# A planner's choice of PSUM banks and the order of the first loads in a fused three-layer decoder kernel

## The chip, the cores and the metric

One NeuronCore of a Trainium2 chip runs the whole kernel. The metric is the device time of one execution in microseconds (us). Three executions of the kernel before took 1398.2 to 1399.92 us, median 1399.54 us. One further execution was taken with the hardware profiler: 1397.8 us, of which its trace spans 1396.1 us.

The engines are named as in the profile: PE is TensorE (matmuls; PEld its weight loads), DVE is VectorE, ACT is ScalarE, POOL is GpSimd, SP is SyncE, which here only issues DMAs. Each engine works through its own queue in order. They meet at semaphores: every engine counts its finished steps, and another engine waits until that count is reached.

## What is computed

For each of 16 batch items (512 rows of 256 numbers) three blocks are added to the running x:

```python
x = x + nystrom_attention(layernorm(x))        # 16 heads, 64 landmarks
x = x + cross_attention(layernorm(x), ctx, mask) # 16 heads, 64 keys
x = x + expert_ffn(layernorm(x))               # 1 of 8 experts, chosen by the item's last row

# nystrom_attention, per head: q_l, k_l are means over 8 rows each
attn1 = softmax(q @ k_l.T); attn2 = softmax(q_l @ k_l.T); attn3 = softmax(q_l @ k.T)
V = attn2
for _ in range(6):
    KV = attn2 @ V
    V = 0.25 * V @ (13 * I - KV @ (15 * I - KV @ (7 * I - KV)))
out = attn1 @ (V @ (attn3 @ v))

# expert_ffn
h = gelu(x @ W1[sel] + b1[sel]); y = h @ W2[sel] + b2[sel]
x = x + 0.3 * (y @ Wo + bo)
```

All of it is in float32. The products W2[e] @ Wo of the eight experts are formed once at the start (the "fusion", steps `f.0` to `f.7` and `fb`) and stored to memory.

## The kernel before, in words

The work is cut into named steps, each belonging to one engine and one batch item. A step's name has its kind and indices: `t1.1` is the second half of the scores of attention 1, `iT.2`, `iZ.2`, `jT.2`, `jZ.2` are the four matmul groups of the third of six iterations, `e1.1.3` an exponential of ACT that empties the fourth bank of `t1.1`. Three texts list the order of all steps by hand: `FIRST` for the start, `TURN` for the repeated part, `LAST` for the end. A turn holds the first attention of one item, the cross-attention and the expert of older items, and the projections of the next (the suffix -1, -2, -3 says how far back), so that PE always has another item's work between two dependent steps. `S` steps issue DMAs on SP, `P` steps are PE's, `A`, `D` and `G` those of ACT, DVE and POOL. `program()` unrolls the lists into `PROGRAM`.

PSUM has eight banks of 128 x 512 float32. Every PE step writes 1, 2 or 4 of them (`banks_of`), and a named step of ACT or DVE empties each (`emptied_by`). `plan()` walks through `PROGRAM` once and gives out the banks: a list `free` holds the free banks in the order in which they were emptied, in program order over all engines, and each step takes from the front, `free.pop(0)`. `BEFORE` keeps which step emptied the bank last. In the PE block, `body` turns this into waits: `emptied` is the count of ACT and of DVE that must be reached before the banks may be written, and each kind adds what its operands need, through `due` (operand and bank of one engine in one wait) or `unmet` (operand alone). `first` leaves a wait out where PE has already waited for as high a count of that engine. A step has 0 to 3 waits: 244 steps have none, 596 one, 407 two and 44 three, 1542 waits in all. The first `wait_ge` of a step rides on its first weight load, the others are an instruction of their own ahead of it, which can hold two.

At the start SP issues the first x, then, in the same step `S.x@0`, the four constants of the first layer (`FIRST_CONSTS`: wqkv with 768 KB, bqkv with 3 KB, bv and bout with 128 KB each), then w2.2 (512 KB, one expert's matrix for the fusion), then the fusion's own constants (`fc`: wfo with 256 KB, b2T and bfo with 8 KB each), then the other matrices. PE's first step is `f.2`, which needs w2.2 and `fc`. DVE's step `nmA` of item 0 and POOL's `xr` wait for `FIRST_CONSTS`, and the load of the second x (`S.x@1`) waits for both.

Lines of the profile: matmuls of `chain` are L1322 (projections, fusion, expert), of `spread_out` L1331 (`iT`, `iZ`), of `bring_home` L1341 (`jT`, `jZ`); `t1` and `tx` begin with L1562, `t3` with L1447, `s1` is L1530, `xnTb` and `xnTc` are L1397, `a` is L1477 and L1479. DVE's `wb` is L1152, `recx` the RECIPROCAL L1218, `y` L1182; ACT's `az` is L940, `q` L874, `h` L1006, `e3` L896, `ex` L959; POOL's `kbd` is L691.

Of the kernel before, what the change touches and what calls it, by code (L numbers as in the profile page):

```python
# [13 lines left out]
P = 128  # L14
# [47 lines left out]
    S.x@0 S.w2.2@0 D.lnA@0 S.fc@0 P.f.2@0 S.w2.3@0 S.w2.1@0 P.f.1@0 P.f.3@0 G.lnA@0 D.nmA@0 A.f.2@0  # L62
# [216 lines left out]
def emptied_by(engine, step):  # L279
# [12 lines left out]
    if engine == "D":  # L292
# [10 lines left out]
        if kind in ("v", "s2", "mT3", "z", "o1", "w1", "vx", "ox", "wx", "logit", "y3", "fb"):  # L303
# [4 lines left out]
OPERANDS_FROM = {"q": "A", "k": "A", "v": "A", "s3": "A", "x2T": "D", "mT3": "D", "t3": "AD", "zT": "AD", "z": "A",  # L308
# [3 lines left out]

# [16 lines left out]

def plan():  # L330
# [20 lines left out]
def decoder_kernel(nc, a, out):  # L351
# [9 lines left out]
    with ExitStack() as ctx:  # L361
# [130 lines left out]
        passed = {}  # L492

        def first(eng, sem_, n):

            if passed.get((eng, sem_), 0) >= n:
                return False
            passed[eng, sem_] = n
# [7 lines left out]
        def due(eng, who, emptied, i, *steps):  # L506

            n = max(emptied[who], *[DONE[who, i, s] for s in steps])
            return n if first(eng, done[who], n) else 0
# [136 lines left out]
        def _(pool):  # L646
# [186 lines left out]
            run("G", body)  # L833
# [3 lines left out]
        def _(act):  # L837
# [177 lines left out]
            run("A", body)  # L1015
# [3 lines left out]
        def _(dve):  # L1019
# [291 lines left out]
            run("D", body)  # L1311
# [3 lines left out]
        def _(pe):  # L1315
# [35 lines left out]
            def body(i, step):  # L1351
# [6 lines left out]
                if "D" not in OPERANDS_FROM.get(kind, ""):  # L1358
                    if first(pe, dve_done, emptied["D"]):
                        pe.wait_ge(dve_done, emptied["D"])  # L1360
                if "A" not in OPERANDS_FROM.get(kind, ""):
                    if first(pe, act_done, emptied["A"]):
                        pe.wait_ge(act_done, emptied["A"])
                o = tile(i, step)
                if kind == "kx":
                    all_consts(pe)
                    g = slice(8 * LM * n, 8 * LM * (n + 1))
# [3 lines left out]
                elif kind == "vx":  # L1371
                    all_consts(pe)
                    if first(pe, ctx_loaded, 16 * (i + 1)):
                        pe.wait_ge(ctx_loaded, 16 * (i + 1))
                    for r in range(2):
                        last = chain(o[64 * r:64 * r + 64, 0:P],
                                     [(ctxT[:, k, :], wv[:, k, r * P:(r + 1) * P]) for k in range(KD)])
                elif kind == "xnTa":
                    if i == 0:
                        if c := due(pe, "D", emptied, 0, ("nmA",)):  # L1380
                            pe.wait_ge(dve_done, c)
                    elif c := unmet(pe, "G", i, ("lnA",)):
                        pe.wait_ge(pool_done, c)
                    for t in range(T):
                        last = nc.tensor.transpose(o[:, t * P:(t + 1) * P], xn["a"][:, t, n * P:(n + 1) * P], ident[:])  # L1385
                elif kind in ("xnTb", "xnTc"):
                    x = kind[-1]
                    if x == "b" and n == 0:
                        if c := unmet(pe, "G", i, ("lnB", 0)):
                            pe.wait_ge(pool_done, c)  # L1390
                    else:
                        if c := due(pe, "A", emptied, i, ("nmB",) if x == "b" else ("nmC", n)):
                            pe.wait_ge(act_done, c)
# [291 lines left out]
```

## Time and profile before

| | |
|---|---|
| median of three executions | 1399.54 us (1398.2 to 1399.92) |
| the profiled execution | 1397.8 us, span of its trace 1396.1 us |
| mean granted TensorE clock | 0.998 |
| PE busy | 1355.2 us (97%) |
| PEld busy | 889.7 us (64%) |
| DVE busy | 1029.5 us (74%) |
| ACT busy | 667.0 us (48%) |
| POOL busy | 571.1 us (41%) |
| PE's share of the chain that ended last | 85% |

The page gives one execution. Busy times are the union of an engine's instructions; the ends of matmuls are modelled and overlap the next ones, so a short stall of PE, up to some 0.2 us or more after a matmul of 512 columns, doesn't show as idle time. It shows in the starts: equal steps have equal distances from start to start, and a longer distance is a wait. The timeline merges instructions of one line that follow each other; "x2" with 0.77 us are two instructions that together take 0.77.

### The profile page before, as it was taken

The numbers are of one execution on the slowest core, as the hardware profiler recorded it, in microseconds if no ns is written. First come the engines' busy times: TensorE is split into PE (matmuls) and PEld (weight loads), VectorE is DVE, ScalarE is ACT, GpSimd is POOL, SyncE is SP. The second block draws the span as 40 slices with busy tenths as digits, with TensorE's granted clock in tenths as the row PEclk, the third lists the DMA queues.
The fourth block names the chain that finished last, engine by engine and source line by source line (L and its number), as shares of the span: only waits on it lengthen the run. The fifth ranks groups of instructions, "written<-read, shape, count | busy, mean of one in ns | idle before, by whom it ended". The sixth has DMA issues, their size and how long they took to land.

```text
span 1396.1 us, 53472 instructions
## 1 busy us (share of the span) xinstructions
PE 1355.2 (97%) x23732; PEld 889.7 (64%) x23732; DVE 1029.5 (74%) x2194; ACT 667.0 (48%) x1230; POOL 571.1 (41%) x799
## 2 busy tenths in 40 slices
PE   6998999999999999999999999999999999999998
PEld 4756666666766767665666766666666656676555
DVE  3487887758786886878778686877868777898641
ACT  2424355454555546355554644555454544435652
POOL 6223444443626244362534436153353543417132
PEclk9999999999999999999999999999999999999999
DMA  8002010120201011020101101010110100001122
GB/s 285 1 3 95 3 63 3 45 75 3 66 5 51 20 38 33 3 66 5 51 20 37 34 3 58 13 51 20 37 34 3 52 2 19 18 4 39 25 77 65
DMA packets 40536, 53.18 MB, mean 38 GB/s; under 512 B 9698, under 2 KB 30450, under 8 KB 40306
## 3 DMA queue, kind: packets, MB, share of 16 engines
q1 hardware_dynamic: 31602, 41.37, 9.2%
q10 hardware_dynamic: 8704, 8.39, 1.8%
q8 instruction: 187, 3.06, 0.9%
q14 instruction: 43, 0.35, 0.1%
HBM read 37.16 MB, written 12.59 MB: 36 GB/s over the span
## 4 chain that ended last, share of the span: by engine, by line
PE 85%; DVE 5%; ACT 3%; issue 2%; POOL 1%; DMA 1%; DVEq 1%; POOLq 0%; SPq 0%; ACTq 0%
PE bank L1322 41%; PE bank L1575 8%; PE bank L1341 7%; PE bank L1331 7%; PE bank L1564 3%; PE bank L1530 2%; PE bank L1418 2%; PE bank L1397 2%; PE bank L1462 2%; PE bank L1543 2%; PE bank L1451 2%; ACT p3T L896 1%; PE bank L1385 1%; PE bank L1562 1%; PE bank L1424 1%
## 5 line engine op out<-in xcount | busy, mean ns | idle before, releaser
L778 POOL TENSOR_TENSOR b<-ut,eye 128x256 f32<-128x256 f32 x192 | 137.6, 733 | 498.6 <-DVE ut L1161 428.9
L940 ACT ACTIVATE az<-bank 128x320 f32<-128x320 f32 x192 | 67.5, 400 | 185.6 <-PE bank L1331 185.2
L1322 PE MATMUL bank<-xnT_a,wqkv 128*128 128x512 f32 x256 | 123.6, 609 | 0.3 <-ACT xnT_a L864 0.3
L1218 DVE RECIPROCAL oT_x<-bank 128x256 f32<-128x256 f32 x64 | 109.2, 1733 | 19.2 <-PE bank L1575 19.2
L1322 PE MATMUL bank<-w2e,hT 128*128 128x256 f32 x512 | 119.0, 386 | 1.5 <-ACT hT L1006 1.4
L1218 DVE RECIPROCAL oT<-bank 128x256 f32<-128x256 f32 x64 | 111.5, 1747 | 10.6 <-PE bank L1575 10.6
L1322 PE MATMUL bank<-xnT_c,w1e 128*128 128x512 f32 x256 | 117.0, 597 | 1.3 <-DVE m_x L1192 0.9
L1090 DVE TENSOR_REDUCE m<-bank 128x1 f32<-128x512 f32 x128 | 82.9, 680 | 38.5 <-PE bank L1418 36.9
L1322 PEld LDWEIGHTS bank<-w2e,hT 128*128 128x128 f32 x512 | 96.0, 192 | 16.9 <-issue 2.7
L896 ACT ACTIVATE p3T<-bank 128x512 f32<-128x512 f32 x128 | 66.7, 603 | 79.1 <-PE bank L1451 78.9
L959 ACT ACTIVATE pT_x<-bank,neg_bias 128x512 f32<-128x512 f32 x128 | 79.9, 696 | 29.8 <-PE bank L1564 28.8
L1152 DVE SCALAR_TENSOR_TENSOR wb<-bank,eye 128x256 f32<-128x256 f32 x192 | 73.1, 411 | 28.5 <-PE bank L1331 27.8
L1192 DVE TENSOR_REDUCE m<-bank 128x8 f32<-128x512 f32 x128 | 81.7, 682 | 15.4 <-PE bank L1530 15.2
L1192 DVE TENSOR_REDUCE m_x<-bank 128x8 f32<-128x512 f32 x128 | 79.5, 680 | 14.6 <-PE bank L1543 14.5
L1170 DVE SCALAR_TENSOR_TENSOR uz<-uz,bank 128x320 f32<-128x320 f32 x192 | 78.3, 435 | 8.2 <-PE bank L1341 5.6
L1341 PEld LDWEIGHTS bank<-wb,az 64*64 64x64 f32 x2560 | 45.5, 134 | 57.9 <-DVE wb L1152 43.9
L1006 ACT ACTIVATE hT<-bank,b1e 128x512 f32<-128x512 f32 x64 | 43.2, 683 | 75.8 <-PE bank L1322 75.5
L1322 PEld LDWEIGHTS bank<-xnT_c,w1e 128*128 128x128 f32 x256 | 46.8, 190 | 49.3 <-issue 44.8
L1331 PEld LDWEIGHTS bank<-uz,ut 64*64 64x64 f32 x3072 | 59.2, 133 | 27.8 <-DVE uz L1170 10.9
L958 ACT ACTIVATE pT<-bank 128x512 f32<-128x512 f32 x128 | 68.5, 604 | 16.6 <-PE bank L1564 16.5
L685 POOL TENSOR_SCALAR xn_a<-x_in,mv_a,rstd_a 128x256 f32<-128x256 f32 x60 | 72.8, 1228 | 2.7 <-issue 2.5
L1331 PE MATMUL bank<-uz,ut 64*64 64x80 f32 (+1 forms) x3072 | 71.3, 228 | 1.2 <-DVE attn L1120 0.4
(223 smaller groups left out, 2979.2 us busy)
## 6 DMA issues: line engine op xcount, KB each, us to landing
x_in<-in_x SPq DMA_DIRECT2D x16, 512.0 KB, 3.8
w1e<-in_W SPq DMA_DIRECT2D x16, 512.0 KB, 3.5
w2e<-w2o SPq DMA_DIRECT2D x16, 512.0 KB, 4.1
out<-base ACTq DMA_DIRECT2D x32, 256.0 KB, 2.1
row_e<-w2o_row SPq DMA_DIRECT2D x16, 128.0 KB, 4.6
hT<-in_W2T SPq DMA_DIRECT2D x2, 512.0 KB, 6.5
pT_x<-in_ctxT SPq DMA_DIRECT2D x1, 1024.0 KB
ctxT<-in_ctxT SPq DMA_DIRECT2D x16, 64.0 KB, 2.6
```

The source lines that it names most:

```text
L778: return g.tensor_tensor(b7[:, q, :], ut[:, q, :], eye[28 if it else 7][:].unsqueeze(1) .broadcast_to([P, 4, LM]), ALU.subtract).then_inc( ...
L896: return s.activation(p3T[:, j].rearrange("p t c -> p (t c)"), tile(i, ("t3", k), j)[:], ACT.Exp).then_inc(act_done, 1)
L959: return s.activation(pT[x][:, 4 * k + j, :], src, ACT.Exp, bias=neg_bias[:, i:i + 1]).then_inc(act_done, 1)
L1090: return v.tensor_reduce(m3[:, k, j:j + 1], tile(i, ("s3", k), j)[:], AX.X, ALU.max).then_inc(dve_done, 1)
L1152: return v.scalar_tensor_tensor(wb[:, h], src, 1.0 / 16 if it else 1.0, eye[15][:].unsqueeze(1).broadcast_to([P, 4, LM]), ALU.mult, ALU.ad ...
L1170: return v.scalar_tensor_tensor(uz[:, q, lo:], uz[:, q, lo:], 3.25 if it else 13.0, src[:, :, lo:], ALU.mult, ALU.subtract).then_inc(dve_d ...
L1192: return v.tensor_reduce(m[x][:, :, j, 2 * k:2 * k + 2], tile(i, ("s" + x, k), j)[:].rearrange("p (t h c) -> p t h c", t=T, h=2), AX.X, AL ...
L1218: return v.reciprocal(oT[x][:, k, cols], tile(i, ("den" + x, k))[:, cols]).then_inc(dve_done, 1)
L1322: last = mm(dst, lhsT, rhs, start=(k == 0), stop=(k == len(pairs) - 1))
L1331: last = mm(tile(i, step, r)[64 * c:64 * c + 64, w * j + lo:w * j + hi], lhsT[q, j + 4 * c, 0:LM], rhs[q, j + 4 * c, lo:hi], start=True, s ...
L1341: last = mm(tile(i, step, c)[64 * r:64 * r + 64, w * j + lo:w * j + hi], lhsT[q, r, j, 0:LM], rhs[q, r, j, lo:hi], start=True, stop=True)
L1575: last = mm(o[rows(j), :], w, pT[x][:, 4 * n + j, :], start=True, stop=True)
```

## The change

It has two parts. `plan()` no longer takes the front bank: it looks at the first three free banks and takes the one with the lowest price, where `operands(step)` says what the step waits for anyway. In the PE block, `counts` replaces `due`: it leaves out a wait that is implied by another one, through `reached`, which records what each step of another engine had itself waited for. And in `FIRST`, `S.fc` moves ahead of `S.w2.2`, and the four `FIRST_CONSTS` become a step `S.qc` behind it. The listed order of all other steps stays.

```diff
 FIRST = """
-    S.x@0 S.w2.2@0 D.lnA@0 S.fc@0 P.f.2@0 S.w2.3@0 S.w2.1@0 P.f.1@0 P.f.3@0 G.lnA@0 D.nmA@0 A.f.2@0
+    S.x@0 S.fc@0 S.w2.2@0 D.lnA@0 S.qc@0 P.f.2@0 S.w2.3@0 S.w2.1@0 P.f.1@0 P.f.3@0 G.lnA@0 D.nmA@0 A.f.2@0
...
+def operands(step):
+
+    kind, n = step[0], step[1] if len(step) > 1 else 0
+    if kind in ("q", "k", "v"):
+        return [("A", ("xnTa", 0)), ("A", ("xnTa", 1))]
...
+    if kind in ("t1", "tx"):
+        return [("A", ("mT" + kind[1],))]
...
 def plan():
 
     done, count = {}, {}
     bank, before = {}, {}
     free = [(b, None) for b in range(BANKS)]
+    waited = {"A": 0, "D": 0}
     for engine, i, step in PROGRAM:
         if step[0] != "out":
             count[engine] = done[engine, i, step] = count.get(engine, 0) + 1
         if engine == "P":
+            asked = set()
+            for who, name in operands(step):
+                if done[who, i, name] > waited[who]:
+                    waited[who] = done[who, i, name]
+                    asked.add(who)
             for j in range(banks_of(step)):
-                bank[i, step, j], before[i, step, j] = free.pop(0)
+                price = [0 if emptier is None or done[emptier] <= waited[emptier[0]] else
+                         1 if emptier[0] in asked else 2 for _, emptier in free[:3]]
+                bank[i, step, j], emptier = free.pop(price.index(min(price)))
+                before[i, step, j] = emptier
+                if emptier and done[emptier] > waited[emptier[0]]:
+                    waited[emptier[0]] = done[emptier]
+                    asked.add(emptier[0])
...
+        def counts(eng, emptied, i, **steps):
+
+            need = {"A": emptied["A"], "D": emptied["D"], "G": 0}
+            for who, names in steps.items():
+                need[who] = max([need[who], *[DONE[who, i, s] for s in names]])
+            mine = passed.setdefault(eng, {})
+            need = {who: n for who, n in need.items() if n > mine.get(done[who], 0)}
+            left = {who: n for who, n in need.items()
+                    if not any(reached[other, m].get(done[who], 0) >= n for other, m in need.items())}
+            for who, n in left.items():
+                for sem_, m in (*reached[who, n].items(), (done[who], n)):
+                    mine[sem_] = max(mine.get(sem_, 0), m)
+            return {who: left.get(who, 0) for who in need.keys() | set("ADG")}
...
-        def run(who, body):
+        def run(who, eng, body):
             for engine, i, step in PROGRAM:
                 if engine == who:
                     body(i, step)
+                    if (who, i, step) in DONE:
+                        reached[who, DONE[who, i, step]] = dict(passed.get(eng, {}))
...
-                    if i == 0:
-                        for dst, src in FIRST_CONSTS:
-                            sp.dma_start(dst, src).then_inc(first_consts_loaded, 16)
+                elif kind == "qc":
+                    for dst, src in FIRST_CONSTS:
+                        sp.dma_start(dst, src).then_inc(first_consts_loaded, 16)
...
                 elif kind in ("jT", "jZ"):
                     it = n
-                    if c := due(pe, "D", emptied, i, ("wb", it, 0), ("wb", it, 1)):
-                        pe.wait_ge(dve_done, c)
-                    if c := due(pe, "A", emptied, i, ("az", it, 0), ("az", it, 1)):
-                        pe.wait_ge(act_done, c)
+                    c = counts(pe, emptied, i, A=[("az", it, 0), ("az", it, 1)], D=[("wb", it, 0), ("wb", it, 1)])
+                    if c["D"]:
+                        pe.wait_ge(dve_done, c["D"])
+                    if c["A"]:
+                        pe.wait_ge(act_done, c["A"])
```

The other kinds of PE steps are rewritten in the same way.

## Rows read from the trace of the kernel before

**Rows 1.** The page: busy time of PE, and engines of the chain that ended last.

```profile
PE 1355.2 (97%) x23732; PEld 889.7 (64%) x23732; DVE 1029.5 (74%) x2194; ACT 667.0 (48%) x1230; POOL 571.1 (41%) x799
...
PE 85%; DVE 5%; ACT 3%; issue 2%; POOL 1%; DMA 1%; DVEq 1%; POOLq 0%; SPq 0%; ACTq 0%
```

**Rows 2.** Waits of PE: line, waited for, us in total, times, longest.

```profile
PE bank L1322 <- DMA bfo_row<-in_bfo: 10.7, 1, 10.7
PE bank L1530 <- DVE vt L1082: 2.3, 1, 2.3
```

**Rows 3.** Busy times by stretch: length, engines' us, granted clock, DMA share, GB/s.

```profile
327.00:1080.00 753.00, 749.79 (x13618) 490.90 (x13612) 583.52 (x1247) 377.59 (x696) 319.07 (x424) 1.00 0.10 30
```

**Rows 4.** Timeline, jT.1 and jT.2 of item 7: start, us, engine, instruction, idle before.

```profile
646.85 0.77 ACT L940 ACTIVATE az<-bank 128x320 f32<-128x320 f32 x2 [0.45 <-PE bank L1331]
647.76 0.46 PE L1341 MATMUL bank<-wb,az 64*64 64x64 f32 x15
...
653.21 0.42 DVE L1152 SCALAR_TENSOR_TENSOR wb<-bank,eye 128x256 f32<-128x256 f32 x1 [0.16 <-issue]
653.69 0.69 PE L1341 MATMUL bank<-wb,az 64*64 64x64 f32 x32 [0.39 <-DVE wb L1152]
```

**Rows 5.** Timeline, xnTb of item 7 and of item 15 on PE.

```profile
691.90 1.06 PE L1397 MATMUL bank<-ident,xn_b 128*128 128x128 f32 x8
...
1315.46 1.09 PE L1397 MATMUL bank<-ident,xn_b 128*128 128x128 f32 x8
```

**Rows 6.** Timeline around iT.1 of item 7.

```profile
642.50 3.36 DVE L1218 RECIPROCAL oT_x<-bank 128x256 f32<-128x256 f32 x2
...
645.52 0.69 PE L1331 MATMUL bank<-b,uz 64*64 64x64 f32 x32
```

**Rows 7.** Timeline around t1.1 of item 7.

```profile
652.05 0.40 PE L1562 MATMUL bank<-mT,minus 32*128 32x512 bf16 x4
652.18 0.77 ACT L940 ACTIVATE az<-bank 128x320 f32<-128x320 f32 x2 [3.59 <-PE bank L1331]
```

**Rows 8.** Timeline, t1.1 and the jT behind it, items 8 and 14.

```profile
734.09 0.40 PE L1562 MATMUL bank<-mT,minus 32*128 32x512 bf16 x4
...
735.45 0.69 PE L1341 MATMUL bank<-wb,az 64*64 64x64 f32 x32
...
1182.50 0.40 PE L1562 MATMUL bank<-mT,minus 32*128 32x512 bf16 x4
...
1183.68 0.69 PE L1341 MATMUL bank<-wb,az 64*64 64x64 f32 x32
```

**Rows 9.** Timeline around a and s1.1 of item 8.

```profile
690.09 0.69 ACT L1006 ACTIVATE hT<-bank,b1e 128x512 f32<-128x512 f32 x1
...
690.62 0.27 PE L1477 MATMUL bank<-attn,attn2T 64*64 64x64 f32 x1
...
708.71 1.57 ACT L896 ACTIVATE p3T<-bank 128x512 f32<-128x512 f32 x3
...
710.23 1.17 PE L1530 MATMUL bank<-kbd,qT 32*128 32x128 f32 x32
```

**Rows 10.** Timeline, t3.1 of item 1 and xnTc.0 of item 14.

```profile
114.08 0.40 PE L1447 MATMUL bank<-m3T,minus 32*128 32x512 bf16 x4
114.22 0.93 DVE L1182 TENSOR_SCALAR y_bd<-bank 64x64 f32<-64x64 f32 x4 [0.64 <-PE bank L1521]
...
1347.94 0.66 PE L1397 MATMUL bank<-ident,xn_c 128*128 128x128 f32 x4
...
1348.87 2.42 ACT L959 ACTIVATE pT_x<-bank,neg_bias 128x512 f32<-128x512 f32 x4
```

**Rows 11.** DMA rate in slices of 1.5 us from 0 on; POOL's kbd of item 0.

```profile
GB/s 0 124 330 380 376 363 356 391 403 411 389 384 391 421 415 389 341 338 322 103 0 11 0 0 0 0 0 0 0 0 0 0 0 11 0 5 0 0 0 0
...
32.19 0.76 POOL L691 TENSOR_TENSOR kbd<-ksum,par_mean 128x128 f32<-128x128 f32 x2 [4.57 <-DVE ksum L1073]
```

**Rows 12.** Busy times by stretch, right after the long wait of rows 2.

```profile
1150.90:1154.40 3.50, 3.50 (x41) 2.24 (x38) 3.08 (x7) 0.00 (x0) 0.00 (x0) 0.52 0.00 0
```

More of the change, by code:

```diff
@@ L1374, in body @@
                         pe.wait_ge(ctx_loaded, 16 * (i + 1))
+                    c = counts(pe, emptied, i)
+                    if c["A"]:
+                        pe.wait_ge(act_done, c["A"])
+                    if c["D"]:
+                        pe.wait_ge(dve_done, c["D"])
                     for r in range(2):
@@ L1387, in body @@
                     x = kind[-1]
[L1388 to L1392, printed above, removed]
-                            pe.wait_ge(act_done, c)
+                    c = counts(pe, emptied, i, **({"G": [("lnB", 0)]} if (x, n) == ("b", 0) else {"A": [("nmB",) if x == "b" else ("nmC", n)]}))
+                    if c["D"]:
+                        pe.wait_ge(dve_done, c["D"])
+                    if c["A"]:
+                        pe.wait_ge(act_done, c["A"])
+                    if c["G"]:
+                        pe.wait_ge(pool_done, c["G"])
                     for k in range(KD):
@@ L1426, in body @@
                 elif kind == "x2T":
-                    if c := due(pe, "D", emptied, i, ("soft2",)):
-                        pe.wait_ge(dve_done, c)
+                    c = counts(pe, emptied, i, D=[("soft2",)])
+                    if c["A"]:
+                        pe.wait_ge(act_done, c["A"])
+                    if c["D"]:
+                        pe.wait_ge(dve_done, c["D"])
                     for j in range(4):
@@ L1431, in body @@
                 elif kind == "mT3":
-                    if c := due(pe, "D", emptied, i, ("mp3",)):
-                        pe.wait_ge(dve_done, c)
+                    c = counts(pe, emptied, i, D=[("mp3",)])
+                    if c["A"]:
+                        pe.wait_ge(act_done, c["A"])
+                    if c["D"]:
+                        pe.wait_ge(dve_done, c["D"])
                     for k in range(KD):
@@ L1453, in body @@
                 elif kind == "zT":
-                    if c := due(pe, "D", emptied, i, ("v", 0), ("v", 1)):
-                        pe.wait_ge(dve_done, c)
-                    if c := due(pe, "A", emptied, i, *[("e3", n, j) for j in range(4)]):
-                        pe.wait_ge(act_done, c)
+                    c = counts(pe, emptied, i, A=[("e3", n, j) for j in range(4)], D=[("v", 0), ("v", 1)])
+                    if c["D"]:
+                        pe.wait_ge(dve_done, c["D"])
+                    if c["A"]:
+                        pe.wait_ge(act_done, c["A"])
                     for h in range(2):
@@ L1464, in body @@
                 elif kind == "z":
-                    if c := due(pe, "A", emptied, i, ("zT", 0), ("zT", 1)):
-                        pe.wait_ge(act_done, c)
+                    c = counts(pe, emptied, i, A=[("zT", 0), ("zT", 1)])
+                    if c["D"]:
+                        pe.wait_ge(dve_done, c["D"])
+                    if c["A"]:
+                        pe.wait_ge(act_done, c["A"])
                     for j in range(2):
@@ L1523, in body @@
                 elif kind == "s1":
-                    if c := due(pe, "A", emptied, i, ("q", n)):
-                        pe.wait_ge(act_done, c)
-                    if c := unmet(pe, "G", i, ("kbd",)):
-                        pe.wait_ge(pool_done, c)
+                    c = counts(pe, emptied, i, A=[("q", n)], G=[("kbd",)])
+                    if c["D"]:
+                        pe.wait_ge(dve_done, c["D"])
+                    if c["A"]:
+                        pe.wait_ge(act_done, c["A"])
+                    if c["G"]:
+                        pe.wait_ge(pool_done, c["G"])
                     for t in range(T):
@@ L1546, in body @@
                     x = kind[-1]
-                    if c := due(pe, "D", emptied, i, ("mp" + x,)):
-                        pe.wait_ge(dve_done, c)
+                    c = counts(pe, emptied, i, D=[("mp" + x,)])
+                    if c["A"]:
+                        pe.wait_ge(act_done, c["A"])
+                    if c["D"]:
+                        pe.wait_ge(dve_done, c["D"])
                     for t in range(T):
@@ L1605, in body @@
                         pe.wait_ge(expert_out_loaded, 32 * (i + 1))
-                    if c := due(pe, "A", emptied, i, *[("h", f) for f in range(FM)]):
-                        pe.wait_ge(act_done, c)
+                    c = counts(pe, emptied, i, A=[("h", f) for f in range(FM)])
+                    if c["D"]:
+                        pe.wait_ge(dve_done, c["D"])
+                    if c["A"]:
+                        pe.wait_ge(act_done, c["A"])
                     for t in range(2):
@@ L1614, in body @@
                         pe.wait_ge(w2_loaded[n], 16)
+                    c = counts(pe, emptied, i)
+                    if c["A"]:
+                        pe.wait_ge(act_done, c["A"])
+                    if c["D"]:
+                        pe.wait_ge(dve_done, c["D"])
                     w2T = fused_space(n).rearrange("p (k f) -> p k f", k=KD)
```

234 lines of the change are left out of this document (148 added, 86 removed), and 3 rows, old and new, of the table OPERANDS_FROM.

## The prediction

> **What bounds the kernel now.** I read the page first, then its chain, then PE's waits, then the timeline around single steps. TensorE (PE) is busy 97% of the span and 85% of the chain that ended last [rows 1]. Of its listed waits one is long, 10.7 us before the first matmul, for a constant's DMA; the next, 2.3 us, is a single wait for VectorE (DVE) [rows 2]. Between 327 and 1080 us, where the hand-written turn repeats, PE is busy 749.8 of 753.0 us at full clock [rows 3]. So the end is set by PE's order of work, and whatever delays a PE step there delays the end unless a wait behind it shrinks by as much. The 451 steps with two or three waits are the target of the change; what such a wait costs has to be read first.
>
> **The price of a wait.** A step's first `wait_ge` rides on its first weight load; further ones are an instruction of their own ahead of it. Step jT.2 of item 7 has both, and DVE's `wb` (653.21 + 0.42 = 653.63) came last, on the riding wait: PE starts at 653.69, 0.06 later. In jT.1 the second wait, for ScalarE's (ACT's) `az`, came last (646.85 + 0.77 = 647.62): PE starts at 647.76, 0.14 later [rows 4]. A separate wait that is met last thus costs 0.08 us more. One that was met long ago costs nothing I can see: the two steps xnTb in a row take 1.06 us where the second has two waits and 1.09 where it has one [rows 5].
>
> **Part 1, fewer waits.** Applied to the listed order, the new rule (banks from the first three free, then pruning) leaves 1390 of 1542 PE waits and 356 of 451 steps with two or more. At nearly all of the 95 places the dropped wait was met over 0.15 us before PE came, so they are worth nothing; at three a late one goes: -0.3 us (bounds: 0, and 95 x 0.08 = -7.6). The Trainium skill (Advanced Engine Details and Errata, Sequencer Loop) says that instructions are read and queued while an earlier one waits for its semaphore. No row shows that queue; it would put this term at 0.
>
> **Part 2, other banks.** A bank brings the wait for whoever emptied it last. Before, a step takes the banks freed first. The new rule prices a bank 0 if PE has already waited past its emptier, 1 if that emptier's engine is already waited for by this step, 2 otherwise. It knows only counts, no times: a bank freed much later on an engine that is asked anyway beats one free for long on the other. In a repeated turn four places come out worse, one wait each on PE, with all of PE's work queued behind it (item 7, then 8):
> - iT.1: its second bank was the one ACT's `q` freed at 645.4; now it is the one DVE's `recx.1.1` frees. The two reciprocals end at 642.50 + 3.36 = 645.86, PE can start at 645.92 and started at 645.52: +0.40 [rows 6]. DVE turned next to `wb.1`, which waits for iT.1, so nothing gives this back.
> - t1.1: its fourth bank was the one of `wx.1` (DVE); ACT is asked already, so now it is `az.2.0`. Two `az` take 0.77 from 652.18, the first ends near 652.6; PE starts at about 652.68 and not 652.05: +0.63 [rows 7]. Behind it jT.2 waits for `wb` anyway. Start to start, t1.1 to jT.2 takes 1.64 in item 7, 1.36 in item 8, and 1.18 where nothing is waited for (1182.50 to 1183.68) [rows 4, 7, 8]; so 0.46 or 0.18 comes back. Three of ten turns are like item 7: 10 x 0.63 - 3 x 0.46 - 7 x 0.18 = 3.7.
> - a: its second bank is now that of `h.2`, whose ACT step ends at 690.09 + 0.69 = 690.78: start 690.84 and not 690.62, +0.22 [rows 9]. The next step, xnTb.1 at 691.90, was held by ACT [rows 5] and gives back 0.19: net 0.03.
> - s1.1: now waits for the last `e3` of the half before (708.71 + 1.57 = 710.28): start 710.34 and not 710.23, +0.11 [rows 9].
> Ten turns hold the first two, nine the others: 4.0 + 3.7 + 0.3 + 1.0 = **+9.0 us**. These releases follow PE's own steps by fixed times, so they move with PE.
> In the two irregular stretches (60 to 327 and after 1080 us) the same reading, each new bank's release against PE's start, gives 27 places and +12.4 us. The first large one is t3.1 of item 1: it now waits for `y` of item 0 (114.22 + 0.93 = 115.15; start 115.21 and not 114.08, +1.1). The last is xnTc.0 of item 14: it now waits for the first of four `ex` that take 2.42 us from 1348.87 on (over by about 1349.5; start 1349.6 and not 1347.94, +1.7) [rows 10]. There PE waits often, and I take back 5.1 us where a later wait is for work that does not hang on the delayed step: **+7.3** (bounds +3 and +12.4).
>
> **Part 3, constants.** The first matmul needs w2.2 and the fusion's constants; bytes up to them fall from 2323 KB to 1296 KB (wqkv 768, bv and bout 128 each, bqkv 3 go behind). At 330 to 380 GB/s [rows 11] that is 2.7 to 3.2 us; issue and landing overheads stay, so I take **-2.7** (bounds -1.8, -3.2). What moves back: DVE's `nmA` and the `xr` of GpSimd (POOL), which wait for these constants, SP's S.x@1 behind both, and with it w2.0, w2.4 and the main constants, all by about 2.6 us. The nearest user is on POOL: `kbd` starts at 32.19 after 4.57 idle [rows 11], so a queue 2.6 later still meets it; gone, the cover would cost up to the 2.7 gained.
>
> **The sum.** -0.3 + 9.0 + 7.3 - 2.7 = +13.3 on the profiled execution's 1397.8 us: 1411.1. The median shown, 1399.54, lies 1.7 above that execution: **1412.8 us**.
>
> **The rivals.**
> - *The stalls are absorbed (the other side).* If PE's stalls give DVE and ACT slack, so that `recx.1.1` and `az.2.0` come earlier relative to PE and later waits shrink, the end keeps only the gains: -2.7 - 0.3, 1396.5. For: DVE has 3.36 us of reciprocals in one go [rows 6]. Against: PE busy 99.6% there [rows 3] leaves little wait to shrink. It decides where over 13.3 of the 16.3 us of stalls come back.
> - *Half absorbed.* Irregular places cost nothing and t1.1 half: 1399.5 + 9.0 - 1.9 - 3.0 = 1403.6; still slower. All of it beyond that, down to no change within noise, is the thin case "same".
> - *The clock falls.* After the 2.3 us wait [rows 2] the granted clock was 0.52 for 3.5 us (the lower level, 1.2 GHz): 1.7 us lost [rows 12]. Five new stalls of 1.0 to 1.7 us could each do that: up to +8.5, 1421.3. Against: waits of under 0.5 us between 327 and 1080 left it at 1.00 [rows 3]. The Trainium skill (TensorE: Matmul & The Clock Gate, A second HAM failure mode: psum-queue depth-cycling) tells of short idling between matmul groups, from cycling through banks, that throttles the clock again and again. The trace, with 1.00 over 753 us, speaks against it here.
> - *The early load doesn't come early.* If landing and not bytes sets the first matmul, part 3 is worth 0: 1415.5.
>
> **How the numbers follow.** Forecast, all terms within their bounds (1406 to 1419): 0.70. Clock falls: 0.08, 1421. No early load: 0.07, 1415.5. Half absorbed: 0.03. Absorbed down to within 0.2% (2.8 us, about what a measurement tells from no change): 0.04. Absorbed wholly: 0.08, 1396.5. So slower 0.88, same 0.04, faster 0.08. The range, 1403 to 1421, takes in the first five but for the ends.
>
> **What would show it.** After the change PE's rows for t1.1 should start about 0.06 us after the first `az` ends, iT.1 after the second reciprocal, and PE's listed waits should newly name `az` (ten times, some 0.3 us idle each, since the modelled ends cover the rest), RECIPROCAL and `y`. The first matmul should start near 8.0 us and not 10.66. A turn, now 82.0 us long (t1.1 at 652.05 and 734.09 [rows 7, 8]), should grow by 0.9 us. I am wrong if turns keep their length, or if the first matmul comes no earlier.

## The result and the profile after

Six executions of the changed kernel took 1413.13 to 1418.85 us, median 1416.15 us. Beside them the kernel before took 1399.49 us (median of six). The ratio is 1.012, 95% interval 1.0104 to 1.0136: the change makes the kernel slower by 16.7 us, 3.3 us more than the forecast 1412.8 and inside its range. On another chip (the run "changed again" below) the ratio was 1.0103 (1.0082 to 1.0123). The profiled execution took 1418.07 us, its span is 1416.4 us.

The page and PE's waits answer [rows 1, 2]. Columns of the waits: engine and line, what was waited for, us in total, times, longest.

```profile
PE 1359.9 (96%) x23732; PEld 889.2 (63%) x23732; DVE 1029.8 (73%) x2194; ACT 666.6 (47%) x1230; POOL 569.8 (40%) x799
...
PE 81%; DVE 8%; ACT 6%; issue 2%; DMA 1%; POOL 1%; DVEq 1%; SPq 0%; POOLq 0%; ACTq 0%
```

```profile
PE bank L1374 <- DMA w1e<-in_W2T: 8.2, 1, 8.2
PE bank L1659 <- ACT az L992: 5.6, 10, 0.6
PE bank L1383 <- DVE oT_x L1270: 3.3, 10, 0.3
PE bank L1618 <- DVE vt L1134: 2.2, 1, 2.2
...
PE bank L1456 <- ACT pT_x L1011: 1.6, 1, 1.6
...
PE bank L1527 <- DVE y_bd L1234: 1.1, 1, 1.1
```

PE's share of the chain that ended last fell from 85% to 81%, and DVE and ACT took it. Two waits are new and come ten times each, once per turn: t1.1 (now L1659) waits for `az`, and iT.1 (L1383) for the reciprocals that write `oT_x`. The long wait for `vt` stands as before.

The timeline of item 7 and the next turn's t1.1 answer [rows 6 to 8]:

```profile
649.13 3.36 DVE L1270 RECIPROCAL oT_x<-bank 128x256 f32<-128x256 f32 x2
...
652.55 0.69 PE L1383 MATMUL bank<-b,uz 64*64 64x64 f32 x32 [0.33 <-DVE oT_x L1270]
...
659.20 0.77 ACT L992 ACTIVATE az<-bank 128x320 f32<-128x320 f32 x2 [3.59 <-PE bank L1383]
659.69 0.40 PE L1659 MATMUL bank<-mT,minus 32*128 32x512 bf16 x4 [0.56 <-ACT az L992]
...
660.87 0.69 PE L1393 MATMUL bank<-wb,az 64*64 64x64 f32 x32
...
742.91 0.39 PE L1659 MATMUL bank<-mT,minus 32*128 32x512 bf16 x4 [0.56 <-ACT az L992]
```

Before, t1.1 started 0.13 us ahead of `az`; now it starts 0.49 behind its start, once the first of the two has ended. iT.1 starts 0.06 after the second reciprocal ends (649.13 + 3.36 = 652.49), as forecast. This turn, from t1.1 to the next t1.1, is 742.91 - 659.69 = 83.22 us long and was 82.04: +1.18, where +0.9 was forecast; the mean over nine turns is +1.11. In the irregular stretches the two places named in [rows 10] turned out so:

```profile
113.61 0.39 PE L1527 MATMUL bank<-m3T,minus 32*128 32x512 bf16 x4 [1.05 <-DVE y_bd L1234]
...
1366.06 2.42 ACT L1011 ACTIVATE pT_x<-bank,neg_bias 128x512 f32<-128x512 f32 x4
1366.80 0.66 PE L1456 MATMUL bank<-ident,xn_c 128*128 128x128 f32 x4 [1.60 <-ACT pT_x L1011]
```

The start, on PE:

```profile
8.19 5.08 PE L1374 MATMUL bank<-wfo,w1e 128*128 128x256 f32 x16 [8.19 <-DMA w1e<-in_W2T]
13.91 3.72 PE L1374 MATMUL bank<-wfo,hT 128*128 128x256 f32 x16 [0.64 <-DMA hT<-in_W2T]
```

The first matmul comes 2.47 us sooner than at 10.66 [rows 2], but the second group, f.1, now waits for its own matrix (w2.1, loaded into hT behind the constants; it landed at 13.87). f.1 starts at 13.91 and started at 16.02 before: 2.1 us are kept here, and 2.0 at the third group, f.3.

Counted from start to start of PE's steps, the whole difference of the two traces splits so: start (up to f.3) -2.0 us; from there to den1.1 of item 3 +4.9; the nine turns from there to den1.1 of item 12 +10.0; the rest +7.4. These make 20.3, the difference of the two spans.

### The profile page after: what moved, and what is told of

Same layout as the page of the kernel before. It is cut to its first block, busy times and chain, and to the rows that moved or that the text cites. A ratio compares the mean times of both kernels' runs of the same rounds, so it can differ in the third digit from the quotient of the medians.

```text
span 1416.4 us, 53376 instructions
## 1 busy us (share of the span) xinstructions
PE 1359.9 (96%) x23732; PEld 889.2 (63%) x23732; DVE 1029.8 (73%) x2194; ACT 666.6 (47%) x1230; POOL 569.8 (40%) x799
## 4 chain that ended last, share of the span: by engine, by line
PE 81%; DVE 8%; ACT 6%; issue 2%; DMA 1%; POOL 1%; DVEq 1%; SPq 0%; POOLq 0%; ACTq 0%
PE bank L1374 38%; PE bank L1383 7%; PE bank L1672 7%; PE bank L1393 7%; PE bank L1661 3%; DVE oT_x L1270 3%; PE bank L1618 2%; PE bank L1456 2%; PE bank L1543 2%; PE bank L1531 2%; PE bank L1634 2%; PE bank L1486 2%; ACT p3T L948 1%; ACT hT L1058 1%; ACT attn2T L962 1%
## 5 line engine op out<-in xcount | busy, mean ns | idle before, releaser
L1383 PEld LDWEIGHTS bank<-uz,ut 64*64 64x64 f32 x3072 | 59.2, 133 | 28.8 <-issue 13.0
L1213 DVE SCALAR_TENSOR_TENSOR ut<-ut,bank 128x256 f32<-128x256 f32 x160 | 61.2, 406 | 18.0 <-PE bank L1393 17.9
```

What stands on the lines that cost most here:

```text
L1383: last = mm(tile(i, step, r)[64 * c:64 * c + 64, w * j + lo:w * j + hi], lhsT[q, j + 4 * c, 0:LM], rhs[q, j + 4 * c, lo:hi], start=True, s ...
```

## The experiments

All are whole kernels, each with a ratio to the kernel before on the same chip. The ratio is not always the quotient of the two medians given beside it: they differ by up to 0.0012, and in one run by 0.0023.

**Banks as before** (the bank freed first; pruned waits and early load kept)

```
-                price = [0 if emptier is None or done[emptier] <= waited[emptier[0]] else
-                         1 if emptier[0] in asked else 2 for _, emptier in free[:3]]
-                bank[i, step, j], emptier = free.pop(price.index(min(price)))
+                bank[i, step, j], emptier = free.pop(0)
```

> The changed kernel with the banks chosen as before (the one freed first); the pruned waits and the early load stay. Theory (the bank choice alone costs, through waits that end later): the trace of the changed kernel lost 2.5 us at the first matmul and gave 0.5 back at the wait for the second set of fused weights, pruning is worth 0, so 1399.5 - 2.0 = 1397.5 us, ratio to before 0.9986; no wait of PE for az, and a turn of 82.0 us. Rival (part of the loss is from the moved loads or the rewritten waits): above 1400, ratio 1.001 to 1.006.

Measured: 1394.46 us (nine runs) against 1397.67, ratio 0.9976 (0.9964 to 0.9987). The whole loss is gone with the bank choice, and what is left is a gain of 3.3 us (1.8 to 5.0). The nine turns are 0.63 us shorter than before in all. Its waits:

```profile
PE bank L1372 <- DMA w1e<-in_W2T: 8.0, 1, 8.0
PE bank L1616 <- DVE vt L1132: 2.3, 1, 2.3
PE bank L1391 <- ACT az L990: 1.3, 2, 1.0
```

The wait for `az` that remains is the two waits of jT that the kernel before has too. So the rival, that moved loads or rewritten waits cost something, is out. That the ratio came out below the 0.9986 of the theory is answered by the run with pruned waits alone: pruning was worth more than 0.

**Constants late** (new banks, pruned waits, old order of loads)

```
-    S.x@0 S.fc@0 S.w2.2@0 D.lnA@0 S.qc@0 P.f.2@0 ...
+    S.x@0 S.qc@0 S.w2.2@0 D.lnA@0 S.fc@0 P.f.2@0 ...
```

> The changed kernel with the first layer's constants loaded ahead of the fusion's, as before; new banks and pruned waits stay. Theory (loads and banks add up): changed kernel's 1416.2 + 2.0 = 1418.2 us, ratio 1.013 to 1.0135, first matmul at 10.7 us. Rival (the early start is eaten by later waits, so the load is worth 0): 1416.2, ratio 1.012. Rival (the load is worth the 2.7 us of the prediction): 1418.9.

Measured: 1417.76 us, ratio 1.0143 (1.0127 to 1.0159), against 1.012 and 1.0103 with the early load. By the ratios that is 3.2 or 5.6 us slower, each with more than 3 us of uncertainty: the sign is as expected, the size can't be told from the times. The traces tell it better. f.1 started at 16.02, 15.60, 16.44, 15.87 and 16.30 us in five traces with the late constants (before and four experiments) and at 13.91, 14.18, 13.89, 14.49 and 14.11 in five with the early load: 1.9 us between the means. A sixth trace with the late constants, of the run with one wait ahead, had its first matmul at 11.74 and f.1 at 18.26, before any wait was added; with it the difference is 2.3.

**Pruned waits alone** (banks and loads as before)

```
-                if c := due(pe, "A", emptied, i, ("nmB",) if x == "b" else ("nmC", n)):
-                    pe.wait_ge(act_done, c)
+                c = counts(pe, emptied, i, ...)
+                if c["D"]: ...
+                if c["A"]: ...
```

> The kernel before with the new way of counting waits alone: banks freed first, loads as before. 1504 PE waits instead of 1542, 438 instead of 451 steps with two or more. Theory (a wait met long ago costs nothing): 1399.5 us, ratio 1.000 within 0.0003. Rival (each step with two or more waits costs 0.08 us whatever it waits for): -13 x 0.08 = -1.0, ratio 0.9993, at the edge of what can be told; only a ratio below 0.998 would say that waits have a price of 0.2 us and more.

Measured: 1395.38 us (twelve runs) against 1397.67, ratio 0.9984 (0.9975 to 0.9993): a small gain of 1.0 to 3.5 us. The theory's 1.000 is out, and the rival's 0.9993 is the very end of the interval; its reason, a price for each separate wait, falls with the runs on added waits below. Part of the gain can be seen. In nine turns the step from a to xnTb.1 is 0.10 us shorter: 1.18 (below) where it took 691.90 - 690.62 = 1.28 [rows 5, 9].

```profile
691.91 0.27 PE L1560 MATMUL bank<-attn,attn2T 64*64 64x64 f32 x1
...
693.09 1.10 PE L1454 MATMUL bank<-ident,xn_b 128*128 128x128 f32 x8
```

Before, xnTb.1 waited for ACT's count twice, first for its bank (504) and then for its operand (505). The later count came last, as a separate instruction. One wait for 505 rides. That is 0.86 us in nine turns, of which xnTb.0 behind it gives back 0.03 each: 0.6 net, and the nine turns are 0.63 us shorter in all. The rest is not accounted for. It is smaller than it looks: every execution has its mean granted clock on record, and with the time that the clock took left out of each, the mean gain is 1.3 us (0.5 to 2.1).

**Covered or front** (one price less)

```
-                         1 if emptier[0] in asked else 2 for _, emptier in free[:3]]
+                         1 for _, emptier in free[:3]]
```

> The changed kernel with one price less in the bank rule: a bank whose emptier PE has already waited past costs 0, all others 1, so without such a bank among the first three the one freed first is taken. 1450 PE waits, 407 steps with two or more; 496 of the step's banks have another emptier than before (707 in the changed kernel). Theory (only a bank freed late costs, and a bank that PE has waited past cannot be late): no new stall, as with the banks of before, 1397.5 us, ratio 0.9986, equal to the run with the banks freed first. Rival (any departure from the order of freeing costs, by holding other steps' banks): 496 of 707 of the loss, some 12 us over that run, 1410, ratio 1.007.

Measured: 1393.72 us against 1397.67, ratio 0.9973 (0.9961 to 0.9985). This can't be told from the run with the banks freed first (0.9976), though it changes the emptier of 496 banks; the nine turns are shorter by 0.64 us as there. Departing from the order of freeing is harmless as long as the other bank's emptier has already been waited past. What costs the time in the changed kernel is the one distinction between price 1 and price 2: "this engine is asked anyway" says nothing on when.

**t1.1 from the front** (the changed kernel, with one step's banks as before)

```
-                         1 if emptier[0] in asked else 2 for _, emptier in free[:3]]
+                         1 if emptier[0] in asked else 2 for _, emptier in free[:1 if step == ("t1", 1) else 3]]
```

> The changed kernel, where step t1.1 alone takes the banks freed first; everything else as in it. By the trace of the changed kernel t1.1 starts 0.63 us later in each of ten turns (6.26 in all), jT.2 gives 2.55 back, and den1.1, whose exponentials come from t1.1, starts 1.91 later in all; t1.1 of item 13 adds 0.85. Theory (den1.1 hangs on t1.1's delay): all of it goes, 6.26 - 2.55 + 1.91 + 0.85 = 6.5 us faster than the changed kernel, and from the first matmul to den1.1 of item 12 the run is 9.98 - 5.6 = 4.4 us over before between items 3 and 12. Rival (den1.1 is late for a reason of its own): 4.6 us faster, and 6.3 us over before in those ten turns. The times, 1409.5 or 1411.5 where before has 1399.5, hardly tell these apart; the offsets do. No wait of PE for az is left in these turns.

Measured: 1407.25 us against 1396.8, ratio 1.0098 (1.0074 to 1.0121); the medians alone give 1.0075. The times don't separate the theories. The offsets do: over the nine turns the run is 4.8 us over before, where the changed kernel is 10.0 and its second trace 9.8. t1.1 and what hangs on it are worth 5.0 to 5.2 us in nine turns, as the theory with the knock-on has it (by the sites, 5.1 in nine turns), and not 3.5. The step den1.1 comes 1.6 us later in these turns in both traces of the changed kernel and 0.1 earlier here, with the same bank in all of them.

```profile
PE bank L1374 <- DMA w1e<-in_W2T: 8.5, 1, 8.5
PE bank L1383 <- DVE oT_x L1270: 3.3, 10, 0.3
PE bank L1618 <- DVE vt L1134: 2.2, 1, 2.2
```

iT.1's ten waits of 0.3 us stand alone now; those of t1.1 are gone.

**Two long-met waits behind, in every step of items 1 to 15** (the kernel before)

```
+    owed.extend([(dve_done, 1), (act_done, 1)])   # waited for ahead of the step's first matmul
```

> The kernel before with two more waits in every PE step of items 1 to 15 (1200 steps), behind the step's own waits, on counts that VectorE and ScalarE passed in item 0: 3942 PE waits instead of 1542, 1228 steps with two or more instead of 451. Theory (a wait met long ago costs nothing, also as an instruction of its own): 1399.5 us, ratio 1.000 to 1.001. Rival (a separate wait costs its 0.08 us each time): 777 more such steps and more of them in the steps that have some, 1200 x 0.08 = +96 us, ratio 1.07. A price of 0.01 us each would be +12 us, ratio 1.009.

Measured: 1401.91 us against 1396.8, ratio 1.0047 (1.0029 to 1.0065): +6.6 us by the ratio, +5.1 by the medians, with 1200 instructions added. The price of 0.08 us each is far out, but so is zero. More than half of it is the clock: the mean granted clock of these executions was 0.9958 and that of the kernel before beside them 0.9978, 5.9 and 3.1 us lost; with that left out the means differ by 1.7 us (0.9 to 2.5). The rest is not spread: the nine turns, with 720 of the steps, are 2.0 us shorter than before and not longer. What grew in the trace is the idle time of PE for which the profile has no releaser, six times and 6.3 us: three times inside a group of small matmuls (4.3 us), three times ahead of a step's first matmul (2.0 us). Waits, and the longest of the six:

```profile
PE bank L1325 <- issue: 6.3, 6, 2.4
```

```profile
191.16 0.61 PE L1325 MATMUL bank<-qbd,kT 32*128 32x128 f32 x14
194.17 0.82 PE L1325 MATMUL bank<-qbd,kT 32*128 32x128 f32 x18 [2.40 <-issue]
```

After 14 of 32 equal matmuls, with no wait between them, PE stood still for 2.4 us. The kernel before has 0.8 us of such idle time in four places, the changed one 1.3 us in two.

**One long-met wait ahead** (the kernel before)

```
             def body(i, step):
+                if i:
+                    pe.wait_ge(dve_done, 1)
```

> The kernel before with one more wait at the head of every PE step of items 1 to 15 (1200 steps), on a count of VectorE that it passed in item 0. It takes the place on the first weight load, so all of a step's own waits move to an instruction of their own: 2742 PE waits, 998 steps with two or more. Theory (a wait's price is paid only where it is met last, 0.054 us if it rides and 0.145 if it stands alone): 144 of the steps meet their riding wait last, 144 x 0.09, less where the wait leads by less, is +11.2 us if none is given back, +6 to +11 in all: 1405 to 1411, ratio 1.004 to 1.008, and the growth is even over the ten turns. Rival (a separate wait costs its 0.09 whenever it is there): 547 more such steps, +49 us, ratio 1.035. Rival (place makes no difference, the two latencies were read from unlike steps): 1.000, save for single stalls without a releaser, which came to some 6 us in the run with two waits behind.

Measured: 1418.65 us against 1397.02, ratio 1.0143 (1.012 to 1.0167): +20 us, twice the upper end of what was expected. Half of the theory holds. Some 96 steps start 20 to 110 ns later, 5.9 us in all, and in all ten turns o1.1, which follows on a wait that now stands alone, starts 0.09 us later (0.087 to 0.092). The growth is not even over the turns, as the theory had it (0.5 to 2.6 us a turn). In the trace, 21.6 us longer, 15 us lie inside the groups; f.2 at the low clock for longer and one more fall of the clock are some 2.9 of them, the rest is mostly in small matmuls (t3, jT, jZ, iT, iZ). Part of that is listed as idle, part is hidden by the modelled ends:

```profile
PE bank L1325 <- issue: 8.5, 13, 2.4
```

```profile
752.71 0.34 PE L1325 MATMUL bank<-wb,az 64*64 64x64 f32 x7 [0.15 <-DVE wb L1152]
753.78 0.62 PE L1325 MATMUL bank<-wb,az 64*64 64x64 f32 x25 [0.73 <-issue]
```

Here jT.2 waited for `wb` with a separate instruction, ran seven matmuls, and stopped for 0.73 us. This run adds 588 instructions, half as many as the run with the waits behind, and loses three times as much (19 us against 1.7 with the clock's time left out of both). So it is not the number of instructions alone.

**Two long-met waits behind, only in steps of large matmuls** (the kernel before, 480 steps)

```
-                if i:
+                if i and kind in ("q", "k", "v", "qx", "w1", "wx", "h", "y3", "xnTa", "xnTb", "xnTc",
+                                  "den1", "denx", "o1", "ox"):
                     owed.extend([(dve_done, 1), (act_done, 1)])
```

> The kernel before with the two long-met waits behind the step's own waits only in the 480 steps of items 1 to 15 whose matmuls are large (0.12 us and more each: transposes, q, k, v, qx, w1, wx, h, y3, and the eight matmuls of den and o); 2502 PE waits. The runs with waits in all steps had stalls of PE in the middle of groups of small matmuls, without a releaser (6.3 us in 6 with the waits behind, 8.5 us in 13 with one ahead, 0.84 in 4 before). Theory A (small matmuls run the instruction stream dry, and only waits among them do harm): idle time without a releaser stays below 1.5 us, ratio 1.000 to 1.001. Theory B (any added instruction moves the places at which the stream is refilled, and hits as many bad places): 2.5 us and more of it, ratio 1.002 or above.

Measured: 1400.33 us (twelve runs) against 1398.45, ratio 1.0014 (1.0003 to 1.0025); the time fits either theory, since both bounds overlap it. The idle time without a releaser is 5.3 us in eight places, five of which are in steps that had nothing added (t3.1 of item 1, jZ.2 of items 4 and 8, zT.0 and zT.1 of item 15).

```profile
PE bank L1325 <- issue: 3.8, 7, 0.9
...
PE bank L1329 <- issue: 1.5, 1, 1.5
```

Theory A falls: the waits need not be near the small matmuls. Theory B needs places that the added instructions move, and the traces have them. Number PE's recorded instructions (weight loads, matmuls and waits) in the order of their starts, from 0: in the fourteen traces 38 idle times without a releaser lie inside a group, and all 38 come at a number that leaves 193 or 194 when divided by 256. Of the nine that lie ahead of a step's first matmul, four do. So the stalls sit at a place that comes back every 256 instructions, whatever the matmuls there, and an added instruction moves all later ones. A trace has some 187 such places and most show no stall; in five traces the 256 instructions ahead of one took 3.0 to 7.9 us where it stalled and a median of about 6 where it didn't, so their pace alone doesn't decide. What does stays open.

**Second matrix sooner, and fusion first** (both with "covered or front" banks)

```
     S.x@0 S.fc@0 S.w2.2@0 D.lnA@0 S.qc@0 P.f.2@0 S.w2.3@0 S.w2.1@0 P.f.1@0   (covered or front)
     S.x@0 S.fc@0 S.w2.2@0 D.lnA@0 S.w2.1@0 S.qc@0 P.f.2@0 S.w2.3@0 P.f.1@0   (second matrix sooner)
     S.fc@0 S.w2.2@0 S.x@0 S.w2.1@0 S.qc@0 D.lnA@0 P.f.2@0 S.w2.3@0 P.f.1@0   (fusion first)
```

> The kernel of the run 'covered or front' with the second set of the fusion's weights loaded ahead of the first layer's constants too. In the changed kernel the second matmul group started 0.8 us late for that load. Theory: the wait goes (its 512 KB now land 1027 KB, some 3 us, sooner), the constants land 1.5 us later at 12.4 us, the first layer's transposes are fed at 17.3 and are due at 20.1, so 0.7 us faster than 1393.7 (ratio to before 0.9973): 1393.0, ratio 0.9968. Rival (something behind the constants becomes late: the transposes, or the keys' mask sums on GpSimd): back at or above 1393.7, and a new wait of PE before 60 us.

> The kernel of the run 'covered or front' with the loads in the order fusion's constants, first fused weights, x, second fused weights, first layer's constants, third fused weights. The bytes up to the first matmul's fall from 1296 to 784 KB, at some 340 GB/s 1.5 us: first matmul at 6.6 instead of 8.2 us, and the second group does not wait, so 1.5 + 0.7 = 2.2 us faster than 1393.7: 1391.5, ratio to before 0.9957. Rival (x lands 1.5 us later, and the normalization chain behind it, which took 4.8 us behind the constants, comes after PE is through with the third group at some 18.5 us): xnTa waits, and the gain is 0.7 to 1.5, ratio 0.9962 to 0.9968.

> Once more the kernel with 'covered or front' banks, pruned waits and the fusion's loads ahead of x. Theory (its third group of fused weights started at 16.06 us instead of 17.6 with the early load and 19.4 before, and this is kept): 3.3 us for the start and 1 for pruned waits, ratio 0.9969, below 0.998 with its whole interval. Rival (what the start gains is given back later): 0.998 and above.

Measured: second matrix sooner 1392.5 us, ratio 0.9972 (0.9956 to 0.9988), no gain over "covered or front" that can be told. Its w2.1 landed at 9.85 us, where it landed at 13.13 to 13.87 in the five traces with w2.1 behind the constants, but f.1 started at 14.01, no sooner than theirs. The wait that it was to take away is in one of those five traces only, that of the changed kernel. In the other four f.1 follows f.2 without a gap, as in the second trace of the changed kernel:

```profile
7.81 6.46 PE L1374 MATMUL bank<-wfo,w1e 128*128 128x256 f32 x16 [7.81 <-DMA w1e<-in_W2T]
14.11 3.62 PE L1374 MATMUL bank<-wfo,hT 128*128 128x256 f32 x16
```

What sets f.1's start there is the slow pace of f.2 itself (last section). Fusion first: 1393.07 us, 0.9967 (0.9951 to 0.9982), and again on another chip 1392.38 us against 1397.02, 0.9959 (0.9943 to 0.9974). Its f.1 starts at 12.71 and 11.92, 1.2 to 2.0 us sooner than the 13.89 of "covered or front", and no wait takes its place (the second of the two traces):

```profile
6.73 5.36 PE L1374 MATMUL bank<-wfo,w1e 128*128 128x256 f32 x16 [6.73 <-DMA w1e<-in_W2T]
11.92 3.62 PE L1374 MATMUL bank<-wfo,hT 128*128 128x256 f32 x16
15.38 3.62 PE L1374 MATMUL bank<-wfo,w2e 128*128 128x256 f32 x16
18.83 1.04 PE L1443 MATMUL bank<-ident,xn_a 128*128 128x128 f32 x8
```

The rival, that xnTa waits, is out: it follows f.3 at once. Against "covered or front" the gain is too small for the times, but against the kernel before this version is faster with its whole interval, twice: 3.7 and 4.6 us of medians. It beats both kernels.

**The changed kernel again**

> The changed kernel itself, on the same chip as the two other runs. Theory: 1.012 as measured, or, from the run with late constants (1.0143) less the 1.8 us (0.0013) by which the third group of fused weights started sooner in four runs with the early load, 1.013. Nothing here tells theories apart; it is the measure for the other two.

Measured: 1411.77 us against 1397.02, ratio 1.0103 (1.0082 to 1.0123). Its nine turns are 9.8 us longer than before, the stretch behind them 4.4 us. With the time that the clock took left out of every execution, the means differ by 16.1 us.

## Why the prediction was right, and where its terms were off

**The bound.** PE's order of work sets the end: confirmed. Waits of some tenths of a microsecond at three steps of a turn move the end by their sum.

**Fewer waits**, -0.3 forecast. Too small. The trace of the pruned kernel gives 0.6 us in nine turns at xnTb.1 and xnTb.0 alone, the times 1.0 to 3.5. The step that failed is the reading of [rows 5]: I compared the lengths of the xnTb groups and not the distance from the step ahead, and looked for dropped waits that were late, not for late waits that begin to ride. The rule of the Trainium skill (Advanced Engine Details and Errata, Sequencer Loop), that instructions are read and queued while an earlier one waits, put this term at 0. The runs agree only in part. In the nine turns of the run with waits behind, the instructions added to 720 steps cost nothing, but that trace has 4.3 us of idle time inside groups of matmuls, which the rule doesn't hold.

**Repeated turns**, +9.0 forecast. Summed by site over ten turns (nine for a and s1.1), the trace of the changed kernel gives iT.1 +3.96 (forecast 4.0), t1.1 +6.26 less 2.55 at jT.2 = 3.71 (3.7), a +1.82 less 1.67 at xnTb.1 = 0.15 (0.3), s1.1 +0.97 (1.0): 8.8 where 9.0 was forecast (xnTb.0 adds 0.26). What I missed is den1.1, +1.8 in ten turns. It waits for the exponential e1.1.3, which reads what t1.1 writes and starts as late as t1.1 does. I followed the give-back of t1.1's delay on PE, at jT.2, but not the delay's way over ACT to the next PE step but three. The run with t1.1 from the front shows it: with t1.1 on time den1.1 is on time.

**Irregular stretches**, +7.3 forecast. Outside the nine turns and the start the trace has 4.9 + 7.4 = 12.3 us. Of that the clock took 3.4 more than before (below). That leaves 8.9; the forecast for the same stretches, with the tenth turn's 0.8, was 8.1. In the second trace, whose clock cost as much as that of before, it is 4.9 + 4.4 = 9.3. The two large ones came as worked out: t3.1 of item 1 idles 1.05 us (forecast +1.1), xnTc.0 of item 14 1.60 (+1.7). The give-back of 5.1 us was estimated with no row for each place, and it was too large by some 1 us.

**Early load**, -2.7 forecast, 1.9 kept (f.1, mean of five against five). Two steps failed. The bytes over the rate gave 2.7, and the first matmul came 2.2 us sooner (means 10.30 and 8.07; the 2.47 of the one pair holds some spread of single executions). And I asked who is behind the first matmul on DVE, POOL and SP, and not on PE itself, which loses 0.3 more. In the changed kernel's trace the next group's matrix was late, 0.8 us by the starts (0.64 listed as idle); in the other four with that order it was not. There f.2 ran at the low clock somewhat longer (last section), and w2.1, landed 0.4 to 1.0 us ahead of f.1's start, would have been the next limit. The cover that I named, POOL's wait ahead of `kbd` [rows 11], held: no wait for it appeared.

**The sum.** Together: start -2.0, nine turns +10.0, irregular +8.9, clock +3.4 make 20.3 for the two profiled executions; without the clock's part it is 16.9, and the medians differ by 16.7. The forecast +13.3 was right in sign and mechanism, and some 3.5 us too small, all its errors going the same way: den1.1 and the rest of the nine turns (1.8), the irregular places (0.8), the early load (0.7) and the -0.3 for fewer waits, which the sum of the traces doesn't show apart. The forecast's fifth case, absorbed down to within 0.2%, would have ended at or below 1402.3 us and so outside the range of 1403 to 1421 that was said to take it in.

**The rivals.** *Absorbed*: out; with the banks as before the 16.7 us come back and a gain of 3.3 remains, so nothing of the nine turns was absorbed. *The clock falls*: it fell, but at the two places where it had fallen before, and longer. Windows of before, of the changed kernel and of the kernel with t1.1 from the front (length, busy times of the engines, granted clock, DMA share, GB/s):

```profile
1150.00:1156.00 6.00, 6.00 (x110) 3.89 (x114) 3.77 (x10) 0.75 (x2) 0.00 (x0) 0.72 0.00 0
1368.00:1374.00 6.00, 5.65 (x21) 4.55 (x22) 0.54 (x4) 1.39 (x4) 3.11 (x4) 0.72 0.28 90
```

```profile
1164.00:1172.00 8.00, 8.00 (x134) 5.18 (x130) 4.33 (x12) 1.97 (x2) 0.00 (x0) 0.57 0.01 2
1386.00:1393.50 7.50, 6.75 (x20) 5.48 (x21) 0.59 (x5) 2.28 (x5) 3.66 (x5) 0.54 0.24 70
```

```profile
1140.00:1165.00 25.00, 22.22 (x458) 13.86 (x458) 21.60 (x40) 10.36 (x19) 9.84 (x12) 1.00 0.01 3
1355.00:1400.00 45.00, 40.98 (x178) 26.47 (x170) 15.31 (x28) 14.38 (x22) 12.10 (x12) 1.00 0.28 82
```

A clock of 0.72 over 6 us costs 6 x 0.28 = 1.7 us, twice, 3.4 in all; the changed kernel's two stretches cost 8 x 0.43 = 3.4 and 7.5 x 0.46 = 3.4, in all 6.8, so 3.4 more. Its second trace has one stretch, of 3.4. The third kernel has t3.1's and xnTc.0's new stalls as well (1.1 and 1.2 us) and the 2.2 us wait for `vt`, and no fall in these stretches. So such stalls need not bring the clock down, and where it falls and for how long differs from one execution to the next. Nor is the clock where the loss is: left out of every execution on the second chip, it leaves 16.1 us. *No early load*: out, by the first matmul. *Half absorbed*: out; the give-back of t1.1 was what the rows said.

## What to carry to other kernels

A planner that knows only counts must not prefer one unmet wait to another: that an engine is asked anyway says nothing on when the count is reached. Taking a buffer whose release has already been waited past, and else the oldest, removed waits without a new stall (0.9973, against 0.9976 with the oldest always: no faster that can be told); anything beyond that needs the times of the trace. When a step is delayed, follow its result through the other engines to the later steps of the bounding one, not only the next step on its own queue, since a delay that seems given back can return there.

## What the hardware showed that I had not expected

PE can stand idle with no release to wait for: 0.8 us in four places before, 6.3 in six, 8.5 in 13 and 5.3 in eight with more wait instructions in its stream, a part of them ahead of a step's first matmul. The stall is no price per instruction. It comes at a few places, each 0.15 to 2.4 us, and most often in the one run whose late waits stood alone; why there is not settled. Where it can come is: all 38 stalls inside groups, in fourteen traces, sit at the one place in every 256 instructions of PE described above. That the next block of instructions is late there is the plain reading, but no trace shows the instructions being fetched.

At the start PE runs at half pace although the column of the granted clock reads 1.00. Windows of before:

```profile
12.00:14.00 2.00, 2.00 (x6) 1.57 (x5) 1.11 (x4) 0.00 (x0) 1.71 (x6) 1.00 1.04 402
...
16.00:18.00 2.00, 2.00 (x11) 1.75 (x10) 0.00 (x0) 1.09 (x2) 1.63 (x7) 1.00 1.07 384
```

Six matmuls of one form are in the first window and eleven in the second. The column is no witness here: the trace's record of the clock begins only at 14.38 us, and what lies ahead of it prints as 1.00. The starts of the matmuls tell the rest. In f.2 they are 0.427 us apart up to that record and 0.216 behind it, and so it is in all fourteen traces: the one distance between the two paces is always the one in which the record begins. So the first matmuls ran at the lower level, 1.2 GHz, and the record begins where the clock rises to 2.4. f.2 had been running for 2.8 to 6.1 us by then, differently in each execution, and half of that time is lost: from f.2's start to f.1's it takes 3.45 us, the pace of the next group, plus that half, to within 0.06 us in thirteen traces (5.13 to 6.52 us in all). The fourteenth, the changed kernel's, has its wait for w2.1 besides. The Trainium skill (TensorE: Matmul & The Clock Gate, Part 1: The HAM clock gate) says that an engine without work stands at 1.2 GHz and is raised to 2.4 once it has been busy, and the traces agree, with 0.427 and 0.216 us. For an early load this means that the first groups of matmuls are no fixed time: compare the start of a later group, over several traces.
